# The silus of conv and gate in one ScalarE instruction each, and the first y product of each half on ScalarE

## The reference

```python
x = x + 0.5 * ffn(layernorm(x))
x = x + attn(layernorm(x))      # a state space block, see below
x = x + 0.5 * ffn(layernorm(x))

# ffn (weights rounded to -1, 0, 1 times a scale)
hidden = silu(x @ Wup.T) * (x @ Wgate.T); out = hidden @ Wdown.T

# state space block, E = 1024 channels, N = 16 states
r = x * rsqrt(mean(x * x) + eps) * norm_w
skip, x_in = r @ W_skip, r @ W_in
xc = silu(causal_conv4(x_in) + conv_b)
delta = softplus(xc @ W_delta_1 @ W_delta_2 + b)
B, C = xc @ W_B, xc @ W_C
h[l] = h[l-1] * exp(delta[l] * A) + (delta[l] * xc[l]) * B[l]   # per channel and state
y[l] = sum over states of h[l] * C[l]
out = resid + ((y + xc * W_D) * silu(skip)) @ W_out
```

## Time and profile before

| | us |
|---|---|
| median of 3 runs | 2800.23 |
| lowest, highest | 2799.28, 2802.76 |
| profiled execution, first to last instruction (span) | 2796.2 |
| busy: PE, DVE, POOL, ACT | 2614.3, 2447.7, 2382.1, 1879.0 |

### The profile page before, as it was taken

How to read it: one execution, slowest core, us unless ns; L and a number is a source line. 1 busy time by engine, 2 the same in 40 slices (tenths; PEclk the granted TensorE clock), 3 DMA queues, 4 the chain that set the end, 5 groups by cost and what they waited for, 6 DMA issues and landing times.

```text
span 2796.2 us, 51718 instructions
## 1 busy us (share of the span) xinstructions
PE 2614.3 (93%) x17439; PEld 2021.6 (72%) x17439; DVE 2447.7 (88%) x3221; ACT 1879.0 (67%) x4340; POOL 2382.1 (85%) x2023
## 2 busy tenths in 40 slices
PE   5776899999999999999999999999999999999878
PEld 4555677777878777786777778677777877776655
DVE  4378899999999999899999999899999999999892
ACT  7374867676676767667676766767676676767651
POOL 1168899999898999999998999999999898999881
PEclk9898999999999999999999999999999999999989
DMA  7013222223222322222232222222222222222220
GB/s 274 31 55 72 60 61 76 56 58 83 59 74 60 80 50 65 77 63 73 58 81 53 70 69 63 73 63 75 54 72 66 66 69 65 73 57 68 64 55 8
DMA packets 94446, 192.44 MB, mean 69 GB/s; under 512 B 12588, under 2 KB 32232, under 8 KB 93672
## 3 DMA queue, kind: packets, MB, share of 16 engines
q0 software_dynamic: 20304, 73.93, 13.7%
q1 hardware_dynamic: 73880, 115.21, 13.0%
HBM read 106.26 MB, written 8.91 MB: 41 GB/s over the span
## 4 chain that ended last, share of the span: by engine, by line
POOL 41%; PE 32%; issue 12%; DVE 7%; ACT 2%; DMA 1%; POOLq 1%; DVEq 0%; ACTq 0%
POOL h L778 22%; PE ps L1596 10%; POOL h L795 7%; PE ps L1607 6%; PE ps L1619 6%; POOL hl L884 4%; PE ps L1553 4%; PE ps L1668 4%; DVE h L1342 3%; POOL u L892 2%; POOL delta L849 2%; DVE xc L1400 1%; PE ps L1629 1%; POOL h L784 1%; POOL xw L799 1%
## 5 line engine op out<-in xcount | busy, mean ns | idle before, releaser
L778 POOL TENSOR_TENSOR h<-u,bb 128x1024 f32<-128x1024 f32 x512 | 1257.8, 2466 | 27.2 <-DVE u L1417 14.2
L1342 DVE TENSOR_TENSOR_SCAN h<-ps,h 128x512 f32<-128x512 f32 x1024 | 1191.8, 1207 | 36.5 <-POOL h L784 18.6
L1037 ACT ACTIVATE ps<-delta,a_neg 128x255 f32<-128x255 f32 x2048 | 873.1, 468 | 377.0 <-DVE h L1342 374.8
L1596 PE MATMUL ps<-xh,q_up 128*128 128x256 f16 x2048 | 466.5, 275 | 36.1 <-DVE xl L1280 19.1
L1364 DVE SCALAR_TENSOR_TENSOR y<-ps,ccur,y 128x512 f32<-128x512 f32 x678 | 471.4, 738 | 6.9 <-PE ps L1553 6.3
L1596 PE MATMUL ps<-xh,q_gate 128*128 128x256 f16 x2048 | 462.7, 273 | 8.1 <-DVE xw L1433 7.8
L1596 PE MATMUL ps<-xl,q_up 128*128 128x256 f16 x2048 | 466.5, 275 | 0.0
L1596 PE MATMUL ps<-xl,q_gate 128*128 128x256 f16 x2048 | 462.4, 273 | 0.0
L1553 PE MATMUL ps<-ident,h 128*128 128x128 f32 x2968 | 398.2, 277 | 50.2 <-DVE y L1364 46.7
L1553 PEld LDWEIGHTS ps<-ident,h 128*128 128x128 f32 x2968 | 344.6, 142 | 112.7 <-issue 50.9
L884 POOL TENSOR_TENSOR hl<-act,hh 128x512 f16<-128x512 f32 x256 | 314.5, 1229 | 97.3 <-ACT hh L1064 94.4
(11 more groups left out here) (126 smaller groups left out, 3642.9 us busy)
## 6 DMA issues: line engine op xcount, KB each, us to landing
xw<-h POOLq DMA_DIRECT2D x141, 512.0 KB, 4.5
bb<-b_scratch SPq DMA_DIRECT2D x224, 256.0 KB, 3.1
cplane<-c_scratch SPq DMA_DIRECT2D x141, 128.0 KB, 3.1
xs<-in_L_attn_resid_dram SPq DMA_DIRECT2D x17, 512.0 KB, 3.5
out_dram<-xs SPq DMA_DIRECT2D x15, 512.0 KB, 4.3
wraw<-in_L_ffn_W_up_dram SPq DMA_DIRECT2D x4, 1024.0 KB, 9.6
wraw<-in_L_ffn_W_gate_dram SPq DMA_DIRECT2D x4, 1024.0 KB, 12.3
wraw<-in_L_ffn_W_down_dram SPq DMA_DIRECT2D x4, 1024.0 KB, 14.1
```

The lines of the kernel that those rows point to most:

```text
L778: ins = pl.tensor_tensor(hs, u[:, :, :], bb[:, q % 2, s % PLANES:s % PLANES + 1, :].broadcast_to([P, HE, CH]), ALU.mult)
L1037: ins = ac.activation(abar[r][:, e, 1:], delta[:, k, 1:], ACT.Exp, scale=a_neg[:, k, n:n + 1])
L1342: v.tensor_tensor_scan(hr, abar[r].rearrange("p e t -> p (e t)"), hr, 0.0, ALU.mult, ALU.add).then_inc(scanned, 1)
L1596: ins = te.matmul(pp[:, f * CH:(f + 1) * CH], w[:, d, col:col + P], part[:, d, :], start=(d == 0 and part is xh), stop=(d == DB - 1 and pa ...
```

## The change

The silus of conv and gate are made by ACT alone, with its silu function: `conv_silu` works in place on `xc`, and `skip_silu` writes `gz` from PSUM and frees the bank. DVE's two multiplies go. The halving of the conv weights and bias goes, and the factor of the output projection is 1.0 in the place of 0.5. The first y product of each half moves from DVE (L1361) to ACT (`y_begin`, a copy with the column of C as its scale). The tanh of the hidden units stays. The tables of slots are the same, and the orders of PE, POOL and SP too.

```diff
-            def conv_tanh(ph, i, half):
+            def conv_silu(ph, i, half):
...
-                need(sc, xc_ready, 2 * c + turn(half))
-                ac.activation(tmp_h, xc[:, half * HE:(half + 1) * HE, :], ACT.Tanh).then_inc(ctanh_ready, 1)
+                xx = xc[:, half * HE:(half + 1) * HE, :]
+                ac.activation(xx, xx, ACT.Silu).then_inc(xc_ready, 1)
...
+            def y_begin(ph, i, s):
+
+                half, n, rows = s // N, state_of(s), rows_before(i, s)
+                need(sc, c_copied, i + 1)
+                if half == 1 or ph == "loop" or ph == "last":
+                    for q in (2 * (1 - half), 2 * (1 - half) + 1):
+                        bk, before = job_no(ph, i, f"YT_{q}")
+                        need(sc, bank_ready[bk], before + 1)
+                for t in range(TB):
+                    need(sc, hT_ready, 2 * rows + t + 1)
+                    ac.activation(y[:, t, :], hT[:, t, :], ACT.Copy, scale=ccur[:, t, n:n + 1]).then_inc(y_added[t], 1)
...
-            def skip_tanh(ph, i, q):
+            def skip_silu(ph, i, q):
                 bk, pp = ready(ph, i, f"SK_{q}")
-                ac.activation(gz[:, 2 * q:2 * q + 2, :].rearrange("p e t -> p (e t)"), pp, ACT.Tanh,
-                              scale=0.5).then_inc(gtanh_ready, 1)
+                ac.activation(gz[:, 2 * q:2 * q + 2, :].rearrange("p e t -> p (e t)"), pp, ACT.Silu).then_inc(bank_used[bk], 1)
...
+                    done = step_of(ph, i, s - Y_BEGIN_LAG)
+                    if done and done[1] % N == 0:
+                        y_begin(ph, *done)
...
-                    if s % N == 0:
-                        ins = v.tensor_scalar(yy, hT[:, t, :], cc, None, ALU.mult)
-                    else:
-                        need(ve, y_added[t], rows)
-                        ins = v.scalar_tensor_tensor(out=yy, in0=hT[:, t, :], scalar=cc, in1=yy, op0=ALU.mult, op1=ALU.add)
-                    ins.then_inc(y_added[t], 1)
+                    need(ve, y_added[t], rows)
+                    v.scalar_tensor_tensor(out=yy, in0=hT[:, t, :], scalar=cc, in1=yy, op0=ALU.mult,
+                                           op1=ALU.add).then_inc(y_added[t], 1)
...
-            def conv_silu(i, half):
-                c = i + 1
-                need(ve, ctanh_ready, 2 * c + turn(half) + 1)
-                xx = xc[:, half * HE:(half + 1) * HE, :]
-                v.scalar_tensor_tensor(out=xx, in0=tmp_h, scalar=1.0, in1=xx, op0=ALU.add, op1=ALU.mult).then_inc(xc_ready, 1)
...
-            def skip_gate(ph, i, q):
-                need(ve, gtanh_ready, QT * i + q + 1)
-                bk, pp = ready(ph, i, f"SK_{q}")
-                gg = gz[:, 2 * q:2 * q + 2, :].rearrange("p e t -> p (e t)")
-                v.scalar_tensor_tensor(out=gg, in0=gg, scalar=1.0, in1=pp, op0=ALU.add, op1=ALU.mult).then_inc(bank_used[bk], 1)
...
-                    add_to_stream(ph, i, name, pslot, 0.5)
+                    add_to_stream(ph, i, name, pslot, 1.0)
```

More of the change, by code:

```diff
@@ L267 @@
 NEXT_LN = 29
+Y_BEGIN_LAG = 1
 EDGES_AT = 0
@@ L577, in macaron_kernel @@
         conv_begun, conv_step, edge_added = sem("conv_begun"), sem("conv_step"), sem("edge_added")
-        ctanh_ready, xc_ready, xw_ready = sem("ctanh_ready"), sem("xc_ready"), sem("xw_ready")
+        xc_ready, xw_ready = sem("xc_ready"), sem("xw_ready")
         sp_step, delta_ready, u_ready = sem("sp_step"), sem("delta_ready"), sem("u_ready")
-        gtanh_ready, z_ready = sem("gtanh_ready"), sem("z_ready")
+        z_ready = sem("z_ready")
         pool_go, dve_go, act_go = sem("pool_go"), sem("dve_go"), sem("act_go")
@@ L756, in scan_columns @@
                 pl.tensor_scalar(a_neg[:, :, :], a_neg[:, :, :], -1.0, None, ALU.mult).then_inc(a_done, 1)
-                pool.wait_ge(vec_step, 2)
+                pool.wait_ge(vcol_ready, 1)
             def u_times_b(i, s):
@@ L1018, in _ @@
             sum_abs(2, 2)
-            sc.wait_ge(vec_step, 2)
+            sc.wait_ge(vec_step, 1)
+            sc.wait_ge(vcol_ready, 1)
             def second_half_saved():
@@ L1181, in evacuate @@
                     elif name[:2] == "SK":
-                        skip_tanh(ph, i, int(name[3]))
+                        skip_silu(ph, i, int(name[3]))
                     elif name == "DT":
@@ L1236, in run @@
                         if after(ph, f"IN_{2 * half + 1}", 1, s):
-                            conv_tanh(ph, i, half)
+                            conv_silu(ph, i, half)
                     for r in range(2 * QUARTERS):
@@ L1317, in _ @@
             ve.wait_ge(vcol_ready, 1)
-            v.tensor_scalar(vcol[:, DB:DB + (TAPS + 1) * EB], vcol[:, DB:DB + (TAPS + 1) * EB], 0.5, None,
-                            ALU.mult).then_inc(vec_step, 1)
             x_low("fill", -1, 1, 0)
@@ L1346, in y_add @@
                 S, half, n = STEPS * i + s, s // N, state_of(s)
-                if s == 0:
+                if is_elem(i, s) or s % N == 0:
+                    return
+                if s == 1:
                     need(ve, c_copied, i + 1)
[L1349 to L1354, removed]
                 rows = rows_before(i, s)
@@ L1416, in first_u @@
                 ve.wait_ge(delta_ready, 1)
+                ve.wait_ge(xc_ready, 2)
                 v.tensor_tensor(u[:, :, :], dd, xc[:, 0:HE, :], ALU.mult).then_inc(u_ready, 1)
-            def skip_gate(ph, i, q):
-                need(ve, gtanh_ready, QT * i + q + 1)
-                bk, pp = ready(ph, i, f"SK_{q}")
-                gg = gz[:, 2 * q:2 * q + 2, :].rearrange("p e t -> p (e t)")
-                v.scalar_tensor_tensor(out=gg, in0=gg, scalar=1.0, in1=pp, op0=ALU.add, op1=ALU.mult).then_inc(bank_used[bk], 1)
             def y_plus_x(ph, i, q):
@@ L1489, in use @@
                     add_to_stream(ph, i, name, pslot, down_sc[:, 0:1])
-                elif name[:2] == "SK":
-                    skip_gate(ph, i, t)
                 elif name[:2] == "YT":
@@ L1502, in background @@
                         conv(ph, i, q)
-                for half in range(2):
-                    if after(ph, f"IN_{2 * half + 1}", 1, s):
-                        conv_silu(i, half)
                 if "T1_0" in has and s == (NEXT_LN_FILL if ph == "fill" else NEXT_LN):
```

## The result

| | before | after |
|---|---|---|
| median of 4 runs each, us | 2800.57 | 2878.37 |
| lowest, highest | 2799.28, 2802.76 | 2871.18, 2880.6 |
| profiled execution, span | 2796.2 | 2875.6 |
| mean granted clock | 0.979 | 0.974 |

The ratio is 1.0274 (95% interval 1.0260 to 1.0289): the change costs 77.8 us. The forecast was 2852, +52; the time lies inside the range, 26 us above the forecast. The profiled execution of after took 2877.44 us, 1.8 more than its span.

A forecast was written before the change was run, and what follows sets the result against it. PE and POOL, both nearly full, and a few waits were taken as the bound. Per chunk 3.7 (gate stall) + 0.5 (y) - 0.6 (relief) = 3.6 us, 14 chunks: +50, edges +2, so 2852 us; range 2812 to 2885.

The forecast's parts named there:

- The stall at the gate: Five new loads in ACT's gate stretch (9.74 to 14.5 us) make PE stand still 3.7 us per chunk, bounds 2.3 and 5.6.
- the rival of the dearer switch: At the gate, changing to the silu table costs as much again as the load: 90 us more, 2942; 3%.
- The conv silus hidden: The conv silus' loads run while ACT would wait for conv or scan: cost 0, or 2.8 us per chunk without cover.
- The relief: Work removed from DVE shrinks PE's wait at the conv: -0.6 us per chunk, bounds 0 and -2.7.
- the relief rival: The gate stall is absorbed and PE's waits for DVE shrink, 38 us at most, half kept: 2781; 8%.
- the cancelling one: Rival: PE's stall at its lower bound of 2.3 us per chunk and as much relief from DVE: 2800; 5%.
- The y products: First-half products on ACT go ahead of `hh`, which POOL awaits: +0.5 us per chunk, bounds 0 and +1.1.
- PE's clock and busy time as before: Expected sign on PE: new waits for ACT, together 3 to 4 us per chunk, but clock and busy time unchanged.
- The edges: Fill, first and last chunk have the same switches with waits beside them: +2 us, bounds -5 and +12.
- The POOL rival: Late `hh` from the y products and at the gates both fall on POOL: 5.1 us per chunk, 71, 2876; 20%.

The follow-up runs named there:

- the third experiment: The changed kernel with the conv as before (tanh on ACT, multiply on DVE), gate silus and first y products on ACT, 165 loads: 2884.04 us, 1.0302.
- the one switch of the kernel before: The kernel before plus an unused one-column silu behind SK_0's tanh in each loop chunk, 93 loads: 2850.48 us, 1.0176.
- the pair: The changed kernel, but in the loop SK_0's silu is held back and goes with SK_1's, 199 loads: 2826.76 us, 1.0092.
- two-switch kernels: The changed kernel with tanh for both silus, save SK_0 and SK_1 in the loop, which keep silu, 121 loads: 2824.97 us, 1.0076.

## Why the prediction was right in kind and 26 us short

The spans by place, us (idle and busy of PE between the first and last copy of C in the loop, read as above):

| | ahead of it | PE idle | PE busy | behind it |
|---|---|---|---|---|
| before | 323.0 | 35.3 | 2077.9 | 360.0 |
| all tanh, y on DVE | 317.7 | 30.3 | 2076.2 | 360.0 |
| all tanh, y on ACT | 318.7 | 40.2 | 2077.1 | 359.3 |
| after | 324.3 | 83.6 | 2097.4 | 370.3 |

From each row to the next are the three terms of my sum: relief -12.0, y +11.1, loads +80.3; together +79.4. (By medians -16, +10 and +82: one profile differs from a median by a few us.)

*The stall at the gate: right.* The chain on ACT (14.60 for 14.5), the places on PE and 3.8 us for 3.7 came out. But 0.4 of the 3.8 is the y products'. The loads make 43.4 us of idle in 13 periods, 3.3 a chunk, as PE's slack takes a part of the first switch. A load costs its 1.3 us: the rival of the dearer switch is out. The drain of about 1380 ns of the Trainium skill ("ScalarE: Activation LUTs", What ACT_TABLE_LOAD costs) is not in these rows either; the prediction's estimate with such a cost was near 2942.

*The conv silus hidden: right in the loop*, shown by the conv silu alone, whose loop is as short as that of the all-tanh kernel with y on DVE (2106.8 for 2106.5), and in line with the third experiment.

*The relief: near in size, and that by luck.* With all tanh and y on DVE the loop is 6.7 us shorter than before, idle and busy, 0.5 a chunk for 0.6. But the wait that I took the 0.6 from, for `xc` at the conv, is still there (3.9 us over six chunks, for 3.7). It goes only where the y product has left DVE, and other waits come for it. The conv silu alone shortens the loop by the same (6.4 us), so that the gate's multiplies add nothing in the loop: the gain comes with the conv's multiply. That multiply also costs POOL time, which I had at nothing. POOL's product takes 3.3 us where it overlaps it, as in before here, and 2.4 else:

```profile
1240.23 3.34 POOL L778 TENSOR_TENSOR h<-u,bb 128x1024 f32<-128x1024 f32 x1
...
1243.84 2.36 POOL L778 TENSOR_TENSOR h<-u,bb 128x1024 f32<-128x1024 f32 x1
```

```profile
1240.01 1.34 DVE L1409 SCALAR_TENSOR_TENSOR xc<-tmp,xc 128x1024 f32<-128x1024 f32 x1 [0.66 <-ACT tmp L1097]
```

That the gain reaches PE by this way is argued, not shown. Ahead of the loop the relief is 5.3 us more, which I had only in the bounds of the edges. That DVE can't win back the stall held: the relief rival and the cancelling one are out.

*The y products: mis-sized.* 0.5 a chunk was halved by an argument on POOL; runs give 10 to 17 us in all, about 0.7 to 1.2 a chunk. The full shift of the upper bound was about right, for another reason: the second half's product, which I had at nothing, costs PE 0.5 us a chunk, and the rest is the first half's. I had also priced the product at 0.58 us for 0.683.

*"PE's clock and busy time as before": wrong, the largest miss.* PE is busy 19.5 us longer in the loop, of which the clock drops are 8 to 15 by the estimates above. I had costed the standstill as idle time only. The drops and the standstill go together over all kernels: 9 in after's loop, 8 and 7 in the two other kernels with three gate switches (conv or y as before), 9 with the one switch of the kernel before, where PE's wait is 2.7 us; in the ten others, before among them, none or a single one. Each of these 33 drops begins at the end of a single standstill of 2.4 to 2.7 us (from 0.5 us before it to 1.3 behind it), and the two single ones (conv silu alone; all tanh with y on DVE) behind one of 2.3 and one of 2.1 us, for `xc`. The standstill alone doesn't decide it, as a part of the chunks has it without a drop. That it is the cause is argued from this order; a filler on PE in the place of the standstill wasn't tried. About 7 us of longer busy time come without a drop (2084.6 in the pair and in the two-switch kernels); I don't know why.

*The edges: mis-sized.* +2 was forecast; the loads cost 5.6 us ahead of the loop and 11.0 behind it, 16.6, inside my bound of +12 only after the relief of 5.3.

By the spans, where 79.4 stand against 52, the difference of 27.4 is 19.5 (PE busy) + 9.6 (edges, 1.3 + 10.3 for 2) - 1.7 (idle in the loop, 48.3 for 50, in which a smaller stall, 3.3 a chunk for 3.7, and dearer y products cancel by luck). The POOL rival named 2876, near the time measured, but by a sum in which PE idles 5.1 us a chunk; it idles 3.7. Of its part on y the size was right.

## What to carry to other kernels

Count the table loads in the order that the compiler makes, and place them: of 162 new loads here the 62 at the conv cost next to nothing, and the hundred at the gate nearly all of the 81 us, because only the latter stand where ACT has no wait. A busy share of 67% says nothing on that; the 10 us of ACT's rows in front of the matmul that waits do. On PE, busy 93%, a repeated stall of 3.8 us cost more than its length, with the clock drops behind it. The same switch cost 9 us in one kernel and 50 in another; in the latter DVE, with a queue behind it, waited for the delayed result. And a multiply that is taken off DVE can be worth what it cost POOL.

## What was not expected of the hardware

The granted clock falls to half for 3.4 us around the end of a single standstill of PE of 2.4 us in the midst of full work: 9 times in after's loop, never in before's.

POOL's time depends on what DVE does beside it. Its 128x1024 product takes 2428 ns on the mean in after:

```profile
L779 POOL TENSOR_TENSOR h<-u,bb 128x1024 f32<-128x1024 f32 x512 | 1238.2, 2428 | 35.0 <-DVE u L1419 16.8 <-issue 6.4 <-POOL u L893 5.0
```

In before it takes 2466. This is not DVE's load in general: with the conv's multiply on DVE the mean is 2459 to 2466 ns, even where DVE is busy only 2367 us (the third experiment), and without it 2428 to 2442, even where DVE is busy 2413 us (conv silu alone). Of the 512 products of before 15 overlap a conv multiply; they take 3.27 us on the mean, the others 2.44. That is 12 us of POOL's time in the run. POOL is busy 2381 to 2382 us in the four kernels with the multiply and 2367 to 2369 in the ten without.
